# Attention with relative positions: row sums from columns of ones, and division between two turns of the result

## The reference

```python
x = _layernorm(src, ln1_g, ln1_b)
q = (x @ wq).reshape(Bs, Ss, H, HD)          # 16 heads of 8
...
ac = jnp.einsum('bihd,bjhd->bhij', q, k)
bd_full = jnp.einsum('bihd,phd->bhip', q, p)  # p: positions
bd = bd_full[:, :, jnp.arange(Ss)[:, None], rel]
att = jax.nn.softmax((ac + bd) * scale, axis=-1)
attn_out = jnp.einsum('bhij,bjhd->bihd', att, v).reshape(Bs, Ss, Ds) @ wo
src = src + attn_out
x2 = _layernorm(src, ln2_g, ln2_b)
sel = jax.nn.sigmoid(x2 @ sel_w)
scores, idx = jax.lax.top_k(sel, K)
```

## Time and profile before

| | |
|---|---|
| time, median of 3 runs | 2733.53 us (2728.04 to 2734.99) |
| profiled execution | 2727.38 us, span 2725.6 us |
| busy of the span: PE, DVE, ACT, POOL | 89%, 71%, 58%, 57% |
| mean granted TensorE clock | 0.964 of full speed |
| steps of the two attention stages | 15 distances each, mostly 33.8 us (first ones) or 34.5 us |

### The profile page before, as it was taken

The page is one execution under the profiler, slowest core; times in us unless marked ns, Lnnn a source line. Parts: engine busy times, 40 slices in busy tenths (PEclk is TensorE's granted clock), DMA queues, the critical chain, the costliest instruction groups (busy, mean ns, idle before and its releaser), DMA issues. The chain is left out here.

```text
span 2725.6 us, 59982 instructions
## 1 busy us (share of the span) xinstructions
PE 2434.7 (89%) x19038; PEld 1833.9 (67%) x19038; DVE 1930.1 (71%) x5169; ACT 1583.6 (58%) x4641; POOL 1556.9 (57%) x2343
## 2 busy tenths in 40 slices
PE   7999799799977999999988988999799999998888
PEld 5788677578865777777776335665577777777733
DVE  5554388455446899999876456776589999987645
ACT  3332245333326999999930226777699999993022
POOL 4322666332325588888743655554567888884365
PEclk9999799899988999999999998999899999999999
DMA  3810366370005455555455126553445555545512
GB/s 121 316 77 1 75 141 141 121 300 1 1 28 134 122 137 140 140 138 135 128 184 152 45 63 141 115 112 83 105 128 134 139 137 137 140 130 176 161 52 64
DMA packets 302396, 326.64 MB, mean 120 GB/s; under 512 B 31718, under 2 KB 274150, under 8 KB 294902
## 3 DMA queue, kind: packets, MB, share of 16 engines
q1 hardware_dynamic: 252934, 280.83, 37.8%
q0 software_dynamic: 12288, 25.19, 3.3%
q10 hardware_dynamic: 36864, 16.79, 2.1%
HBM read 133.36 MB, written 185.01 MB: 117 GB/s over the span
## 5 line engine op out<-in xcount | busy, mean ns | idle before, releaser
L2073 DVE TENSOR_REDUCE a_nm<-a_sr 128x2 f32<-128x512 f32 x256 | 167.0, 685 | 69.9 <-PE a_sr L1805 68.9
L3202 POOL TENSOR_TENSOR f4o_kv<-a5b_room 128x256 f32<-128x256 f32 x192 | 140.2, 731 | 107.7 <-DVE a5b_room L3070 101.9
L3202 POOL TENSOR_TENSOR f6o_kv<-a5b_room 128x256 f32<-128x256 f32 x192 | 140.3, 731 | 98.2 <-DVE a5b_room L3070 92.1
L2973 ACT ACTIVATE f6a_pr<-f6a_sr,f6a_nm 128x256 f32<-128x256 f32 x384 | 181.6, 486 | 12.1 <-DVE f6a_nm L3058 11.2
L2973 ACT ACTIVATE f4a_pr<-f4a_sr,f4a_nm 128x256 f32<-128x256 f32 x384 | 181.6, 486 | 9.2 <-DVE f4a_nm L3058 7.6
L3070 DVE TENSOR_TENSOR a5b_room<-f4a_ur,f4a_turn 128x512 f32<-128x512 f32 x192 | 131.3, 684 | 44.5 <-PE f4a_ur L2815 44.2
L3070 DVE TENSOR_TENSOR a5b_room<-f6a_ur,f6l_turn 128x512 f32<-128x512 f32 x192 | 131.4, 684 | 35.2 <-PE f6a_ur L2815 34.7
L2838 PE MATMUL f4a_sr<-all_ks,all_qs 96*128 96x256 bf16 x512 | 143.7, 281 | 13.9 <-ACT f4a_pr L2973 10.4
L2838 PE MATMUL f6a_sr<-all_ks,all_qs 96*128 96x256 bf16 x512 | 144.1, 282 | 13.2 <-ACT f6a_pr L2973 10.0
L2855 PE MATMUL f6a_tr<-all_table,f6a_pr 128*128 128x128 f32 x1024 | 155.2, 274 | 0.0
L2855 PE MATMUL f4a_tr<-all_table,f4a_pr 128*128 128x128 f32 x1024 | 155.0, 274 | 0.0
(11 more groups left out here) (672 smaller groups left out, 8477.6 us busy)
## 6 DMA issues: line engine op xcount, KB each, us to landing
slots<-f_zero SPq DMA_DIRECT2D x100, 512.0 KB, 6.1
f4a_slide<-f4o_kv SPq DMA_DIRECT2D x64, 383.0 KB
f6a_slide<-f6o_kv SPq DMA_DIRECT2D x64, 383.0 KB
f4o_kv<-f4a_slide SPq DMA_DIRECT2D x64, 256.0 KB
f6o_kv<-f6a_slide SPq DMA_DIRECT2D x64, 256.0 KB
f4o_src<-slots SPq DMA_DIRECT2D x128, 64.0 KB, 2.3
slots<-f4m_y ACTq DMA_DIRECT2D x128, 64.0 KB, 2.4
f6o_src<-slots SPq DMA_DIRECT2D x128, 64.0 KB, 2.2
```

The lines of the kernel that those rows point to most:

```text
L2073: nc.vector.tensor_reduce(nm[:, r // 2, t, at_:at_ + 2], sr[:, g % SB, :].rearrange("p (x s) -> p x s", x=2), AX.X, ALU.max, negate=True). ...
L2973: last = nc.scalar.activation(pr[:, n % 4, x, :], from_, ACT.Exp, bias=nm[:, n % SB, x:x + 1], scale=sign, accum_out=zs[:, b[1], t, h:h + 1])
L3202: nc.gpsimd.tensor_tensor(rr[:, o % RAW, :], tmp[:, o % 2, 0, :], tmp[:, o % 2, 1, :], ALU.add)\
```

## The change

The memory of `vm` gets a one in the unused columns: for rounds 0 and 1 in columns 16 and 17 of each block of 32, for rounds 2 and 3 in columns 0 and 1. Rounds 0 and 1 are now summed in the first half of the bank of `y_ps`, rounds 2 and 3 in the second half, so that the rows of the sums stand beside the results. The exponentials are made without `accum_out`. The reciprocal, the repeat, the two transposes and copy of `rz8`, and the multiply on DVE are gone. In their place:

- slot 4: ACT copies the whole bank of `y_ps` to `y_sb`;
- slot 5: PE transposes it in four pieces ("yt"); DVE takes two reciprocals of 16 columns and makes two products of 128, into `yq`;
- slot 7: PE transposes `yq` back in two pieces ("yb"), ACT copies it to `yn`.

What follows moves later: the "o" product and its addition from slot 6 to 9, the measuring from 7 to 10, POOL's root from 7 to 10, ACT's norm from 9 to 12, x2t from 12 to 14, sel from 14 to 15, the update of `x` from 9 to 13, and `gate_sum` from slot 15 to slot 0 of the next step. The order of the desk is now count, v, yt, yb, xt, o, qk, x2t, sel.

```diff
     def clear(self, dve):
-        nc.vector.memset(self.vm[:, :, :, :, :].rearrange("p a b c d -> p (a b c d)"), 0.0).then_inc(self.vm_zero, 1)
+        whole = self.vm[:, :, :, :, :]
+        nc.vector.memset(whole.rearrange("p a b c d -> p (a b c d)"), 0.0).then_inc(self.vm_zero, 1)
+        dve.wait_ge(self.vm_zero, 1)
+        for first in (16, 2 * C):
+            nc.vector.memset(bass.AP(whole.tensor, whole.offset + first, [list(whole.ap[0]), [QUAD * C, 2 * TT], [C + 1, 2],
+                                                                         [QUAD * HD, QUAD]]), 1.0).then_inc(self.vm_zero, 1)
...
-        AT = {"xt": 8, "qk": 10, "x2t": 12, "sel": 14, "src": 11, "ln": 3}
+        AT = {"y": 4, "yt": 5, "yb": 7, "xt": 8, "o": 9, "qk": 10, "x2t": 14, "sel": 15, "src": 11, "ln": 3}
...
                 if r == 0 and later_than(b, 1):
-                    pe.wait_ge(yn_ready, b[0])
+                    pe.wait_ge(y_copied, b[0])
...
-                        mm = nc.tensor.matmul(y_ps[q, 0:T], vm[:, b[0] % 2, st, r, q], pts[:, r % 2, st, j, :],
+                        mm = nc.tensor.matmul(y_ps[q, r // 2 * T:(r // 2 + 1) * T], vm[:, b[0] % 2, st, r, q], pts[:, r % 2, st, j, :],
...
-                if n == 3 and e:
-                    pe.wait_ge(rz8_ready, e[0] + 1)
-                    out = fill(it, "rz")
-                    for t in range(TT):
-                        mm = nc.tensor.transpose(out[:, t * P:(t + 1) * P],
-                                                 rz8[:, t, :, :].rearrange("p h d -> p (h d)"), k.ident)
-                    mm.then_inc(desk.filled, 1)
...
+                if n == AT["yt"] and e:
+                    pe.wait_ge(y_copied, e[0] + 1)
+                    out = fill(it, "yt")
+                    for hf in range(2):
+                        for t in range(TT):
+                            o = (hf * TT + t) * P
+                            mm = nc.tensor.transpose(out[:, o:o + P], y_sb[:, hf, t * P:(t + 1) * P], k.ident)
+                    mm.then_inc(desk.filled, 1)
+                if n == AT["yb"] and e:
+                    pe.wait_ge(yq_ready, e[0] + 1)
+                    out = fill(it, "yb")
+                    for t in range(TT):
+                        mm = nc.tensor.transpose(out[:, t * P:(t + 1) * P], yq[:, t, :], k.ident)
+                    mm.then_inc(desk.filled, 1)
...
-                    last = nc.scalar.activation(pr[:, n % 4, x, :], from_, ACT.Exp, bias=nm[:, n % SB, x:x + 1], scale=sign,
-                                                accum_out=zs[:, b[1], t, h:h + 1])
+                    last = nc.scalar.activation(pr[:, n % 4, x, :], from_, ACT.Exp, bias=nm[:, n % SB, x:x + 1], scale=sign)
...
+                if n == AT["y"] and e:
+                    act.wait_ge(av_done, (e[0] + 1) * QUAD)
+                    if e[0]:
+                        act.wait_ge(yq_ready, e[0])
+                    copy(y_sb[:, :, :].rearrange("p h t -> p (h t)"), y_ps[:, :]).then_inc(y_copied, 1)
+                if n == AT["yb"] and e:
+                    copy(yn[:, :], taken(it, "yb")[:, 0:T]).then_inc(desk.emptied, 1)
...
-                    if n == 1:
-                        dve.wait_ge(sr.emptied, sr.done(e, NR - 1))
-                        nc.vector.reciprocal(rz[:, :, :], zs[:, par, :, :]).then_inc(rz_ready, 1)
+                    if n == AT["yt"]:
+                        dve.wait_ge(desk.filled, desk.nth(it, "yt"))
+                        bank = desk.bank(it, "yt").rearrange("p (h g c) -> p h g c", h=2, c=QUAD * HD)
+                        for hf in range(2):
+                            last = nc.vector.reciprocal(rz[:, hf, :, :], bank[:, hf, :, 16 * (1 - hf):16 * (1 - hf) + 2])
+                        last.then_inc(rz_ready, 1)
                         dve.wait_ge(rz_ready, i + 1)
-                        nc.vector.tensor_copy(rz8[:, :, :, :], rz[:, :, :].unsqueeze(3).to_broadcast([P, TT, H, HD]))\
-                            .then_inc(rz8_ready, 1)
-                    if n == VALUES - 3:
-                        dve.wait_ge(av_done, (i + 1) * QUAD)
-                        dve.wait_ge(desk.emptied, desk.done(it, "rz"))
-                        nc.vector.tensor_tensor(yn[:, :], y_ps[:, 0:T], rzb[:, :], ALU.mult).then_inc(yn_ready, 1)
-                    if n == 6:
+                        if i:
+                            dve.wait_ge(desk.filled, desk.nth((it[0] - 1, (it[1] + 1) % 2), "yb"))
+                        for hf in range(2):
+                            last = nc.vector.tensor_tensor(
+                                yq[:, :, :].rearrange("p t (j c) -> p (t j) c", c=QUAD * HD)[:, :, 16 * hf:16 * hf + 16]
+                                .rearrange("p g (r d) -> p g r d", d=HD),
+                                bank[:, hf, :, 16 * hf:16 * hf + 16].rearrange("p g (r d) -> p g r d", d=HD),
+                                rz[:, hf, :, :].unsqueeze(3).to_broadcast([P, 2 * QUAD, 2, HD]), ALU.mult)
+                        last.then_inc(yq_ready, 1)
+                        dve.wait_ge(yq_ready, i + 1)
+                        dve.sem_inc(desk.emptied, 1)
+                    if n == AT["o"]:
...
-                    if n == 9:
+                    if n == 13:
                         nc.vector.scalar_tensor_tensor(x_b[:, i, :, :], s1[:, :, :], 0.5, x_b[:, i, :, :],
                                                        ALU.mult, ALU.add)
```

More of the change, by code:

```diff
@@ L2347, in take_values @@
         if i == 0:
[L2348 removed]
+            act.wait_ge(self.vm_zero, 3)
         for t in range(TT):
@@ L2890, in small @@
                     mm.then_inc(desk.filled, 1)
-                if n == AT["xt"] and b:
-                    pe.wait_ge(lead.xn_ready, b[0] * TT + TT)
-                    lead.turn_tokens(pe, b[0], fill(it, "xt")).then_inc(desk.filled, 1)
                 if n == AT["qk"] and b:
@@ L2978, in small @@
                 b, p, e = new(it), prep(it), finish(it)
-                if n == 3 and e:
-                    bank = taken(it, "rz")
-                    copy(rzb[:, :], bank[:, 0:T]).then_inc(desk.emptied, 1)
+                if n == AT["y"] and e:
[5 more added lines that the diff above has]
+                    copy(yn[:, :], taken(it, "yb")[:, 0:T]).then_inc(desk.emptied, 1)
                 if n == VALUES - 3 and p:
@@ L3099, in small @@
                     far.cut(dve, ur_ps[:, 0, :])
+                i = it[0] - 4
+                if n == 0 and 0 <= i < B - 1:
+                    dve.wait_ge(desk.emptied, desk.done((it[0] - 1, (it[1] + 1) % 2), "sel"))
+                    opening.gate_sum(dve, i)
                 i = placed(it)
@@ L3159, in small @@
                         last.then_inc(s1_aggr, 1)
-                    if n == 9:
+                    if n == 13:
                         nc.vector.scalar_tensor_tensor(x_b[:, i, :, :], s1[:, :, :], 0.5, x_b[:, i, :, :],
                                                        ALU.mult, ALU.add)
-                    if n == 15 and kept(e):
-                        dve.wait_ge(desk.emptied, desk.done(it, "sel"))
-                        opening.gate_sum(dve, i)
                 if b:
```

30 lines of the change are left out of this document (14 added, 16 removed).

## The result

The changed kernel takes 2760.85 us (median, 2758.07 to 2762.25) against 2733.82 for the kernel before on the same chip. The ratio is 1.0102, with an interval of 1.0090 to 1.0114. It is slower by 1%, where 2702 us were forecast. The profiled execution has a span of 2758.6 us at a granted clock of 0.962.

What follows compares the result with a forecast made beforehand. No engine alone was taken as the bound, but a loop of waits among DVE, PE and ACT. Late steps -0.85 us and the other terms gave 14.7 less 1.6 a stage, 26.2 in all: 2702 us stated, range 2685 to 2716.

Steps and rivals of the forecast that it cites:

- pieces A to D: Late step's first half, alternating DVE, PE, ACT, PE stretches of 4.85, 4.40, 4.83, 2.93 us; forecast -0.6, -0.22, -0.37, +0.22.
- piece A: DVE's stretch from taking the position terms to the band copy's end, 4.85 us; forecast -0.6 without reciprocal and repeat.
- piece C: ACT's stretch until PE, waiting for exponentials, goes on, 4.83 us; forecast -0.37 for four accumulator reads.
- pieces E and F: Late step's second half, DVE's 12.36 us from slot 8, then PE's 5.08 us; forecast +0.12, 17.56 against 17.44.
- I keep 1.3: Update of x moved to slot 13 beside POOL's same three operations: kept at 1.3 us, bounds 0.4 and 2.5.
- PE has slack there, so I cost it at nothing: PE's "qk" in slot 10 waits 0.8 us for the late "o", costed at nothing as DVE sets that stretch.
- DVE's own queue sets the time: From slot 8 to the step's end, DVE's queued work sets the length: 17.56 us after the change against 17.44.
- The early steps: Three steps a stage with a light DVE, 33.8 us: forecast -1.3 each, PE's work the floor at 32.5.
- The last two steps: Last two steps of each attention stage: forecast to gain 0.8 us each.
- The end behind them: End of each stage, where the last item's new copy, transposes and division have no cover: forecast +1.6 us a stage.
- The slower one: Rival: DVE waits for POOL, update of x 2.3 us and gate_sum 1.2, late step 35.4, 2740 us; chance 0.12.
- ScalarE as the bound: Rival: ACT, busiest engine, bounds every step; a step falls by 2.4 us, giving 2653 us; chance 0.02.

Runs made afterwards that it cites:

- h_third15: Changed kernel with the input's addition ahead of the masks' sums, update of x in slot 14 and the heads' third part in slot 15 instead of 14: 2788.89 us.
- e5: Kernel before with exponentials made without their sums, the tile of sums set to one once: 2716.21 us, ratio 0.9920.
- e4: Kernel before with only the update of x moved from slot 9 to slot 13: 2720.82 us, ratio 0.9949.
- e1: Changed kernel with only the update of x moved from slot 13 to slot 15: 2736.93 us, ratio 1.0010 to the kernel before.
- f_update14: Changed kernel with the update of x in slot 14 instead of 13: 2736.67 us, ratio 1.0001 to the kernel before.
- f_update11: Changed kernel with the update of x in slot 11 instead of 13: 2736.75 us, ratio 0.9997 to the kernel before.
- f_reduce13: Changed kernel with the update of x in slot 13 replaced by a one-input reduction into scratch: 2733.63 us, ratio 0.9988 to the kernel before.
- i_one11: Changed kernel with the input's addition ahead of the masks' sums, update of x in slot 14 and the gate's comparison in slot 11 instead of 12: 2735.29 us.
- the fourth round: Four variants of the changed kernel with early addition, replacing or moving the heads' third part or moving the gate's comparison: 2726.85, 2788.89, 2735.29 and 2731.87 us.
- g_before_update14: Kernel before with only the update of x moved from slot 9 to slot 14: 2723.36 us, ratio 0.9949.
- e2: Changed kernel with the input's addition ahead of the masks' sums and the index in slot 9: 2730.80 us, ratio 0.9993 to the kernel before.
- e3_both: Changed kernel with both the update of x in slot 15 and the input's addition ahead of the masks' sums in slot 9: 2751.69 us, ratio 1.0060.

## Why the prediction was wrong

**The first half: right.** The prediction gave pieces A to D -0.6, -0.22, -0.37 and +0.22, together -0.97. They came to -0.94 in the changed kernel, and the half stayed at 16.05 to 16.14 us in all its variants but h_third15. The reads' -0.37 is confirmed by e5. The other three pieces were not measured one by one, and that the sum is right to 0.03 us is in part luck. In the step after, TensorE waits neither for the band copy of piece A nor for the exponentials of piece C. Its waits in this half fell from 1.13 to 0.41 us and its work from 15.82 to 15.65. The division takes 0.80 us as the earlier trace rows said (1124.88 to the 0.49 of 1125.21, and the gap between). The copy of `y_ps` is hidden. `gate_sum` takes 0.18 us, below the 0.35 assumed.

**The step that failed: pieces E and F.** They were given +0.12 us and took +2.22. Three terms failed. Under all of them lies a reading: the loop went through TensorE's wait of 0.33 us in slot 12 to 13 and passed over the 1.06 us at 1099.08, where TensorE already stood behind the update of `x`.

1. The update of `x`, "I keep 1.3". It took 2.09, below the bound of 2.5 that I had named, but above the 1.9 named as a sign that the forecast was wrong. The reason given, that GpSimd does the same three operations there, was the wrong thing to read. The operations are the same in e4, where it takes 0.58. What goes with the price is at which moment of them the update starts: before, 0.39 us into the second of the three, and after, 0.31 us into the first. The edits e1, f_update14, f_update11 and f_reduce13 show 1.37 us a late step for it, in all 27 us by the steps and 24 by the medians, against the 27.0 by which the changed kernel's median is above that of the one before.

2. "PE has slack there, so I cost it at nothing", of "qk" waiting for the late "o". The wait came at about the size that I gave it (0.72 to 0.99 us against 0.8), and it was not free. VectorE and TensorE wait for each other in this half. Taking it away was worth 0.35 us (18.30 to 17.95, with the update's wait absent in both), 0.34 with the update in slot 14 and 0.08 with it in slot 11. That is neither nothing nor 0.8, and no price of its own: the edit also made the comparison and the third part longer.

3. "DVE's own queue sets the time", with a sum of durations of 17.56 us. That sum has 1.3 for the update. With the 0.41 that it takes without a wait, it is 16.67, and VectorE's busy time in i_one11 is just that, 16.71 us. So the work was reckoned well. What failed is that the queue sets the time: VectorE isn't full in this half (17.17 of 18.30 us in f_update14, 16.71 of 18.21 in i_one11), since it also waits for TensorE's products. Without a wait of the update the half is still 17.95 to 18.31, that is 1.3 to 1.6 us over the sum, and not the last 0.4 us that the fourth round was after. Of that the wait for "qk" explains at most 0.35. What sets the rest stays open. The durations of the update, the comparison and the third part don't, as i_one11 shows.

The loss against the kernel before is clearest between kernels without an update's wait: the second half is 16.79 in g_before_update14 and 18.31 in f_update14, +1.5 us, while the first half is 0.92 shorter. TensorE waits 0.30 us in the one (for exponentials) and 0.74 and 1.01 in the other (for "qk" and for the rotation behind the comparison). So what the change moves into this half (the addition in 9, measuring in 10, the turns for the gate in 14 and 15) costs 1.5 us a late step and its savings in the first half bring 0.9. The update's wait comes on top. How the 1.5 is shared among the moved parts was only tried for the addition.

**The early steps** were given -1.3 and gained 0.96, 0.81 and 0.59. e5 has 32.51, 32.81 and 32.80 us for them without any of the change's other parts. So the reads alone are worth all that was gained there, and the other parts took 0.15 to 0.4 of it back. In the changed kernel TensorE's floor of 32.5 wasn't reached.

**The last steps and the ends of the stages.** The last two steps were given -0.8 each. The last distance took +0.4 in both stages and the last item's own step +1.0 and +1.4. The end behind them was given +1.6 a stage and took +1.95 and +1.90.

**The rivals.** The slower one named the right mechanism, VectorE behind GpSimd, with half of its place: the update at 2.09 instead of the 2.3 it assumed, but the comparison of the gate instead of `gate_sum`. It gave 2740 and a chance of 0.12. It spoke of +0.85 as the point from which the gain is gone, and the second half took +2.1 over its forecast. The rows held a warning that I put aside: an operation with a minimum of 0.415 us and a median of 1.304 has a price set by something else, and each edit that moves it draws that price anew. The range should have reached much further on both sides: the same move made the kernel before 13 us faster.

ScalarE as the bound is ruled out: in e5 2.6 us less of its time brought 0.37 us in a late step's first half and 1.0 to 1.3 in an early step, and the changed kernel's late step grew with 2.0 us less of it. The Trainium skill's rule in "Perfetto Trace Analysis", section "Identifying the Most-Contended Engine", to optimize the engine with the highest occupancy first, names ScalarE here. These traces don't bear it out: ScalarE was the busiest (32.40 of 34.45 us) and the step didn't follow it.

## What to carry to other kernels

Where an operation's median lies far above its minimum in a periodic loop, its duration is no price of its own: read what the other engine does at its start, give the forecast both ends, and try slots in which its partner is idle (here one line moved by four slots was worth 0.5% and the whole rewrite cost 1%). Look for every wait of the engine that the loop goes through, also those inside a piece that another engine seems to hold. A wait of an engine that "has slack" need not be free when two engines hand work to and fro: here 0.74 us of it was worth between 0.08 and 0.35. And an experiment that moves a step changes every meeting later in the loop, so to price its wait alone, replace the operation in its place.

## What the runs showed of the hardware

**VectorE can wait for several operations of GpSimd in a row.** The update's end lay 0.28 to 0.29 us after the end of one of GpSimd's operations in six kernels: after the first (0.58, 0.65 and 0.66 us), the second (1.30 and 1.77) or the third (2.09) of GpSimd's operations that followed one another without gaps from the update's start on. In e2 (0.92) it ended 0.38 after an indirect DMA's issue on GpSimd instead, yet in f_update14, g_before_update14 and f_update11 it took 0.41 beside such an issue. Where it got in after the first, GpSimd's next two were longer (1.75 in place of 1.41 in e4). The Trainium skill states in "SBUF — State Buffer", section "Who interferes with whom", that the loser blocks for the whole instruction. The traces agree that there is a block, but it is not bounded by one instruction. What decides when VectorE gets in isn't shown: the start lay 0.31 us into GpSimd's operation where it waited for three, 0.39 where it waited for two (before), 0.43 and 0.37 where it waited for one, and just ahead of one (0.06) where it waited for two (e3_both).

**The moves don't add.** Two edits worth 1.37 and 1.49 us a late step alone were worth 0.54 together (19.67 to 19.13 in the second half), because the second moved the first one's operation back into GpSimd's row.

**One input doesn't always protect.** A reduction with one input took 0.41 us in the place where the update took 2.09. But a copy from one tile of SBUF into another took 0.90 us throughout the late steps, with 0.42 as its shortest in the same stage.
